# Cross-attention: the layer norm of a group split up and moved into the slots of the group in front, token transposes and Q jobs two slots earlier, residual and context splits moved

## What is computed

```
x = x + attention(layernorm(x))                      # 16 heads of 64, softmax over blocks of 128
x = x + cross_attention(layernorm(x), ctx, ctx, mask)  # 16 heads of 16, keys and values from ctx
x = x + mixture(layernorm(x))                        # 8 experts of 512, summed, gate norm
```

```
Q = x @ Wq.T + bq;  K = ctx @ Wk.T + bk;  V = ctx @ Wv.T + bv
probs = softmax(where(mask, Q K^T / 4, -1e9))
out = (probs V) @ Wo.T + bo
```

## Time and profile before

| | us |
|---|---|
| runs | 952.63, 950.34, 947.82 (median 950.34) |
| the profiled execution | 950.39, of which the trace spans 948.6 |
| cross-attention's first scores | start at 372.56 |
| slot 0 of runs 1, 2, 3 and of the drain (start of S) | 382.76, 429.84, 477.66, 525.71 |
| experts | from about 567 to the end |

### The profile page before, as it was taken

How to read it: one execution, slowest core, us unless ns; L and a number is a source line. 1 busy time by engine, 2 the same in 40 slices (tenths; PEclk the granted TensorE clock), 3 DMA queues, 4 the chain that set the end, 5 groups by cost and what they waited for, 6 DMA issues and landing times.

```text
span 948.6 us, 18374 instructions
## 1 busy us (share of the span) xinstructions
PE 871.0 (92%) x6274; PEld 785.1 (83%) x6274; DVE 567.2 (60%) x1172; ACT 629.4 (66%) x1764; POOL 290.9 (31%) x342
## 2 busy tenths in 40 slices
PE   4899999999999987888988869999999999999997
PEld 3788888889888876787878769999999999999996
DVE  4798888788878865858686856554323332342222
ACT  3797788788778764878787876765454445444543
POOL 2254454445345567546564541000000000000000
PEclk9999999999999999999999999999999999999999
DMA  6310000000000007554444303330000000000000
GB/s 212 105 36 20 1 1 1 0 0 0 0 0 0 1 1 187 114 148 99 144 79 139 75 16 103 92 93 12 22 0 0 0 22 0 0 0 23 1 1 22
DMA packets 21770, 41.98 MB, mean 44 GB/s; under 512 B 3144, under 2 KB 3152, under 8 KB 21712
## 3 DMA queue, kind: packets, MB, share of 16 engines
q1 hardware_dynamic: 21120, 40.91, 16.0%
q10 hardware_dynamic: 592, 0.34, 0.2%
HBM read 30.75 MB, written 10.49 MB: 43 GB/s over the span
## 4 chain that ended last, share of the span: by engine, by line
PE 61%; DVE 17%; ACT 12%; issue 4%; DMA 4%; SPq 1%; POOL 0%; DVEq 0%; ACTq 0%; POOLq 0%
PE Y L482 22%; PE A L482 20%; PE S L482 12%; ACT probs L795 7%; DVE PT L872 3%; PE T L577 3%; DVE nm L962 3%; DVE oraw L981 2%; DVE arena L931 2%; DMA arena<-stage 2%; DMA stage<-arena 1%; DVE st L876 1%; PE O L482 1%; PE O L594 1%; DVE xn L898 1%
## 5 line engine op out<-in xcount | busy, mean ns | idle before, releaser
L872 DVE TENSOR_TENSOR PT<-probs,PT 128x512 fp32r<-128x512 f32 x128 | 89.6, 700 | 231.0 <-ACT PT L852 231.0
L482 PE MATMUL A<-XT,arena 128*128 128x512 f32 x816 | 218.4, 402 | 6.8 <-DVE arena L931 5.5
L795 ACT ACTIVATE probs<-S,nm 128x128 f32<-128x128 f32 x512 | 180.9, 371 | 46.7 <-DVE nm L962 45.1
L482 PEld LDWEIGHTS Y<-arena,PT 128*128 128x128 f32 x1536 | 200.3, 191 | 11.0 <-DVE PT L872 1.1
L482 PE MATMUL Y<-arena,PT 128*128 128x256 f32 x1536 | 204.1, 283 | 0.3
L1185 POOL TENSOR_TENSOR probs<-probs,rinv 128x512 f32<-128x512 f32 x128 | 133.2, 1041 | 215.5 <-DVE rinv L967 213.0
L482 PEld LDWEIGHTS A<-XT,arena 128*128 128x128 f32 x816 | 145.3, 191 | 36.9 <-DVE arena L931 12.4
L852 ACT ACTIVATE PT<-probs 128x512 fp32r<-128x512 f32 x128 | 80.8, 631 | 90.7 <-PE Y L482 90.3
L872 DVE TENSOR_TENSOR PT<-T,PT 128x512 fp32r<-128x512 f32 x128 | 87.6, 684 | 33.9 <-ACT PT L803 31.4
L795 ACT ACTIVATION_READ_ACCUMULATOR probs<-S,nm 128x1 f32 x512 | 107.5, 210 | 0.0
L962 DVE TENSOR_REDUCE nm<-S 128x4 f32<-128x512 f32 x128 | 87.8, 686 | 28.0 <-PE S L569 16.3
(11 more groups left out here) (106 smaller groups left out, 1297.1 us busy)
## 6 DMA issues: line engine op xcount, KB each, us to landing
wst<-in_pieces SPq DMA_DIRECT2D x52, 256.0 KB, 2.7
stage<-arena SPq DMA_DIRECT2D x32, 256.0 KB, 2.3
arena<-stage SPq DMA_DIRECT2D x48, 128.0 KB, 4.0
arena<-stage SPq DMA_DIRECT2D x24, 256.0 KB, 3.8
xs<-in_x SPq DMA_DIRECT2D x4, 512.0 KB, 5.2
craw<-in_ctxT SPq DMA_DIRECT2D x4, 512.0 KB, 3.9
out<-craw SPq DMA_DIRECT2D x4, 512.0 KB, 2.6
rowc<-in_rows ACTq DMA_DIRECT2D x1, 264.0 KB, 5.5
```

The source lines that it names most:

```text
L482: mm = pe.matmul(acc, lhs[a], rhs[b], start=first and i == 0, stop=last and i == 2, skip_group_check=shared)
L795: last = act.activation(probs[:, n % 4, u * P:(u + 1) * P], S[n % 2][:, u * P:(u + 1) * P], ACT.Exp, bias=nm[:, n % 4, u:u + 1], accum_out ...
L872: dve.tensor_tensor(out_, src, hi.bitcast(F32), ALU.subtract).then_inc(sem_, 1)
```

## The change

Tables in the functions `steps` and `run` only, and a `tiles` argument in `stats` and `ln_apply`. For groups 1 to 3 of the cross-attention and for group 0 of the experts:

- statistics: two tiles in slot 10 and two in slot 11 of the run in front (before: four in slot 0); aggregation and the power in its slot 12; `xn` for two tiles in its slot 15 and for two in slot 0 (before: four in slot 1).

For groups 1 to 3 of the cross-attention:

- the token transposes in slots 2 and 3 (before 3 and 5); Q for heads 0 to 7 in slots 4 and 5 (6 and 7), Q for heads 8 to 15 in 6 and 7 (8 and 9), the first half of K for heads 8 to 15 in slot 8 (10), its second half as before in 11.

And: the residual of groups 0 to 2 in slot 7 of the run two further on (before slot 2), its bias in slots 9 and 10 (before 2 and 3); the context split in slots 11 to 14 (before 12 to 15).

```diff
@@ tables @@
-               {0: (0, (0,)), 1: (0, (1,)), 6: (1, (0,)), 7: (1, (1,)),
-                8: (2, (0,)), 9: (2, (1,)), 10: (3, (0,)), 11: (3, (1,))})
+               {0: (0, (0,)), 1: (0, (1,)), 4: (1, (0,)), 5: (1, (1,)),
+                6: (2, (0,)), 7: (2, (1,)), 8: (3, (0,)), 11: (3, (1,))})
-        XT1 = ((3, 4), (3, 5))
+        XT1 = ((3, 4), (2, 3))
+        ALL = tuple(range(TILES))
+        STATS1 = ({0: ALL}, {-6: ALL[:2], -5: ALL[2:]})
+        AGGR1 = (0, -4)
+        NORM1 = ({1: ALL}, {-1: ALL[:2], 0: ALL[2:]})
+        RESIDUAL1 = (QUADS + 6, QUADS + 1)
@@ steps @@
+                at = QUADS - 1 if ph == 0 else RESIDUAL1[g == GROUPS - 1]
+                part = v - SCORES[ph] - at - ((2, 0)[g == GROUPS - 1] if ph == 1 else 1)
+            ahead = ph == 2 or ph == 1 and g > 0
+            if name in ("stats", "norm"):
+                tiles = (STATS1 if name == "stats" else NORM1)[ahead]
+                return [(tiles[v],)] if v in tiles else []
+            if name == "aggr":
+                return [()] if v == AGGR1[ahead] else []
-                return [(g + 1, v - 12)] if ph == 1 and g + 1 < GROUPS and 12 <= v < 16 else []
+                return [(g + 1, v - 11)] if ph == 1 and g + 1 < GROUPS and 11 <= v < 15 else []
@@ run and attentions @@
-                            + [(ph, g, n)]:
+                            + [(ph, g, n)] + [(*e, n - PERIOD) for e in later]:
-            run(order, does, 1, 0, ((0, GROUPS - 1),))
-            run(order, does, 1, 1, ((1, 0),))
-            for g in range(2, GROUPS):
-                run(order, does, 1, g, ((1, g - 1), (1, g - 2)))
+            run(order, does, 1, 0, ((0, GROUPS - 1),), later=((1, 1),))
+            for g in range(1, GROUPS):
+                run(order, does, 1, g, ((1, g - 1), (1, g - 2))[:g],
+                    later=((1, g + 1) if g + 1 < GROUPS else (2, 0),))
```

More of the change, by code:

```diff
@@ L284, in steps @@
                         17: [(1, (2, 3))]}.get(q, [])
[L285 to L293, removed]
+            if name in ("residual", "bias"):
+                at = QUADS - 1 if ph == 0 else RESIDUAL1[g == GROUPS - 1]
+                if name == "residual":
+                    return [()] if v - SCORES[ph] == at else []
+                part = v - SCORES[ph] - at - ((2, 0)[g == GROUPS - 1] if ph == 1 else 1)
+                return [(part,)] if 0 <= part < 2 else []
+            ahead = ph == 2 or ph == 1 and g > 0
[4 more added lines that the diff above has]
+                return [()] if v == AGGR1[ahead] else []
             if name in ("xt0", "xt1"):
@@ L299, in steps, with run @@
             if name == "ctx":
-                return [(g + 1, v - 12)] if ph == 1 and g + 1 < GROUPS and 12 <= v < 16 else []
+                return [(g + 1, v - 11)] if ph == 1 and g + 1 < GROUPS and 11 <= v < 15 else []
             raise ValueError(name)
-        def run(order, does, ph, g, earlier, slots=PERIOD):
+        def run(order, does, ph, g, earlier, slots=PERIOD, later=()):
             for n in range(slots):
@@ L887, in ln_finish, with ln_apply @@
                 dve.tensor_scalar(ve[:, :], mv[:, :, 1], LN_EPS, None, ALU.add).then_inc(ln_var, 1)
-            def ln_apply(ph, g):
+            def ln_apply(ph, g, tiles):
                 dve.wait_ge(ln_rstd, nth(GRP, ph, g, 0))
@@ L893, in ln_apply @@
                     dve.wait_ge(xt_ps, nth(XTE, ph, g, -1))
-                for t in range(TILES):
+                for t in tiles:
                     tile_ = g * TILES + t
@@ L899, in ln_apply @@
                                              ALU.subtract, ALU.mult)
-                last.then_inc(ln_x, 1)
+                if tiles[-1] == TILES - 1:
+                    last.then_inc(ln_x, 1)
             def tokens_lo(ph, g, banks, halves=range(KD)):
@@ L1001, in add_residual, with stats @@
                 last.then_inc(y_read, 1)
-            def stats(ph, g):
+            def stats(ph, g, tiles):
                 if ph == 0:
@@ L1145, in experts @@
                         if m == 28:
-                            ln_apply(2, g + 1)
+                            ln_apply(2, g + 1, range(TILES))
                 if not last:
```

## The result

| | us | |
|---|---|---|
| before | 951.49 (947.82 to 952.95, 4 runs) | |
| after | 938.23 (937.62 to 939.49, 4 runs) | ratio 0.9868, interval 0.9836 to 0.9900 |
| profiled execution after | 937.62, span 935.8 | before 950.39, span 948.6 |

The change makes the kernel about 1.3% faster. The forecast was 934 us, its range 930 to 941: the sign and the range held, and of the 16.5 us that the sum promised the two profiled executions show 12.8.

A forecast was written before the change was run, and what follows sets the result against it. No engine bounds it throughout; some 5 us per run are waits: Q's DRAM trip, layer norm, context. Gains 5.2, 5.0 and 5.25 in runs 1 to 3, drain 2.4, start -1.3: 950.4 - 16.5 = 933.9 us, range 930 to 941.

The forecast's parts named there:

- the DRAM wait: Slot 11's scores wait for Q's 7.8 us trip through DRAM; moved earlier, the wait goes with 2.2 us to spare.
- the lists: Slot prices of TensorE and ScalarE for slots 0 to 15; the larger of each pair sums to 42.3 us a run.
- `xn` in two halves: VectorE, slots 15 and 0: 0.66 us each replaces 1.39 in slot 1, behind the V part in slot 0; costs nothing.
- the context's 0.64: Slot 0: TensorE's K job waits 0.64 us for GpSimd's last context split; moving the split a slot earlier removes it.
- Theory A: Formed after the result: Q's trip is nearly the whole gain; layer norm, V's low part and context split cap slots 0-2 nearly equally.
- The start: Slots 12 to 15 of run 0: power and statistics delay first normalisations (at most 1.6 us) and second maxima; charged 1.3 us.
- The signs: Profile after: no DRAM wait, runs of 42 to 44.3, drain slots 0-2 under 8 us, run 0's first T about 1.3 later.
- rival 1: Transposes and Q halves wait, up to 0.9 us in slot 3, about 0.6 in slots 4, 5; 937 to 938.5; chance 0.23.
- rival 2: Q's DRAM landing grows from 7.8 to 12 us, wait and low clock return, 2.8 a run; 942 us; chance 0.06.
- rival 4: Slower: key and query copies queue on SP, landing doubles to 16 us, a run takes 49.6; 955 us; chance 0.05.
- Rival 3: Slots do not shorten: VectorE's new work in slots 7 and 10-12 delays the maxima; about 945 to 948 us; chance 0.06.
- The rule that I set aside: GpSimd and VectorE's two-port mode exclude each other; `xn` would wait, some 0.25 us each beyond cover, giving 935 us.

The follow-up runs named there:

- Experiment 2: Changed kernel with layer norm, residual and context back in old slots, only Q jobs and token transposes earlier; 938.42 us against 948.98 for the kernel before (0.9886).
- Experiment 9: Changed kernel with transposes, Q and K's first half moved one slot earlier than before instead of two; 941.49 us against 949.9 for the kernel before (0.9912).
- experiment 10: Changed kernel with V ahead of exponentials, aggregation and power in slot 11, group 1's layer norm in its own run; 933.36 us against 949.9 before (0.9830).
- experiment 11: Kernel of experiment 10 with ScalarE's output copy also ahead of the four exponentials; 933.98 us against 949.6 for the kernel before (0.9836).
- experiment 3: Changed kernel with aggregation and power one slot earlier, in slot 11 instead of 12; 938.74 us against 948.98 for the kernel before (0.9891).
- experiment 4: Changed kernel with V's high part ahead of ScalarE's exponentials, its low part ahead of VectorE's output and maxima; 934.69 us against 948.98 before (0.9852).
- experiment 6: Kernel of experiment 4 with the context split back in slots 12 to 15; 935.78 us against 949.9 for the kernel before (0.9852).
- experiment 7: Kernel of experiment 4 with layer norm back in slots 0 and 1; 936.61 us against 949.11 for the kernel before (0.9866).
- experiment 1: Changed kernel with Q jobs and token transposes back in their old slots; 947.17 us against 948.98 for the kernel before (0.998).
- experiment 8: Changed kernel with residual and bias back in their old slots; 937.71 us against 949.6 for the kernel before (0.9874).
- experiment 5: Changed kernel with group 1's layer norm kept in its own run; 936.58 us against 949.9 for the kernel before (0.9861).

## Why the prediction was right, and where it was off

**Right: the DRAM wait and its share.** It was named as the first cap, it is gone from all three runs, and slots 10 to 12 of run 2 went from 11.36 to 7.83. Experiment 2 shows that the queries' half alone gives the result; of some 4.1 us a run 0.7 is slot 9, which lost its second half job, as the lists had it. The lower clock behind the wait went with it, as said. The spare time was near what I gave. In run 2 of the changed kernel Q's low part ends at 447.21, the last copy back lands at 455.22, and the scores of slot 11 start at 457.03: 9.8 us from Q to the scores and 8.0 for the trip (10.0 and 7.8 claimed), so 1.8 to spare against 2.2; in runs 1 and 3 it is 1.8 and 1.3. Experiment 9, which takes a slot away, is 0.63 short in run 1, in accord with it.

**Right in the sum, by luck in its parts: the lists.** Their sum was 42.3 (added up again, 42.4), and experiment 10, with the waits out, has 42.35 and 42.32. Slot 1 was put at 3.1 and slot 2 at 2.83; both are measured to 0.01. Others missed both ways, by 1.25 us up and 1.28 down, and cancelled: the output slots 7, 11 and 15 were put at 2.72 and took 3.0 to 3.06, since O of the next slot waits 0.5 and more for ScalarE's output copy (experiment 11 takes them to 2.55), and slot 5 took 2.64 for 2.4; slots 6, 8 and 12, with a Q or K part, were put at 2.69 and took 2.38, and slot 3 took 3.04 for 3.22. The wait in slots 13 and 14 for aggregation and output, 0.45 by my walk, is 0.48 by experiment 3, all of it in slot 13.

**Wrong: slot 0.** The step that failed is in "`xn` in two halves" and in the list's 2.45 for slot 0: I followed the low part of V on VectorE as something that layer norm stands behind, but not as something that TensorE waits for. O of slot 1 is the first but one to read the new values. The wait was in the trace of before as well, in the open in the drain, where no context split stands in front of it:

```profile
528.27 0.88 PE L482 MATMUL O<-PT,arena 128*32 128x128 f32 x12 [1.25 <-DVE arena L872]
```

In run 2 of before it was hidden by the context's wait, which is of the same height: the low part of V ended at 432.25, O started at 432.40. It is worth 0.83 in runs 2, 3 and the drain, 2.5 of the 4.2 us that are missing in the stage; 1.4 are in slot 0 of run 1 and 0.2 at the start, for other reasons (below). So slots 0 to 3 of a run, which my lists put at 11.6 against 12.77 before, took 12.25, and the drain gave 1.6 in place of 2.4; the context's 0.64 was worth nothing. Experiments 4 and 6 show the two caps on slot 0, experiment 7 that of the layer norm on slots 1 and 2. The layer norm's 0.5 in these slots, less 0.5 in slot 13, came to nothing. Theory A, which put all three on one footing, was wrong in this.

**Off in size: run 1.** I had 41.9, it took 43.26. Its slot 0 lasted 3.88 in place of 2.4, at a granted clock of 0.62 over 384 to 388. The queries' half alone, whose start is as before (10.23) and which does the same work up to there as the kernel before, has 3.77 there at 0.76, where before had 2.36 at 1.00. Nor is it the tables ahead of it: experiments 1, 8 and 9 have those of the changed kernel up to there and took 4.05, 3.28 and 2.73, at 0.57, 0.85 and 0.89, and TensorE has no wait in this slot in any of them. It is when the lower level of the clock (1.2 GHz), which has begun by about 376 in every kernel, ends: at about 385 in experiments 8 and 9, at 387 to 387.5 in the changed kernel and experiment 1. Only experiment 3, whose start is 3 us longer, still has it past 388. What sets the end stays open.

**The start.** 1.3 charged, 1.53 measured, and experiment 5 gives 1.29 of it back. The mechanism was the one named. GpSimd's first normalisation began at 377.89, which is 5.84 behind the first scores against 4.00 before: 1.84 later, more than my bound of 1.6. In experiment 5 it is 0.56 later than before, and the start 0.24 longer.

**The signs.** Two came out a little beside what I had put down: the drain's slots 0 to 2 took 8.05, not under 8, and the first T of run 0 came 1.4 later (6.94 behind the first scores against 5.50), not 1.3.

**The rivals.** The new hand-offs (rival 1) do not show in runs 2 and 3: the first Q half starts at once and slots 2 to 4 exceed the lists by no more than 0.02. In run 1, which has no projections in slots 1 and 2, TensorE is early as I had feared: the second token transposes wait 0.17 for K's low part, and slot 3 lasts 3.37. Rivals 2 and 4 would have needed a longer trip. From the end of Q's low part to the last landing it took 8.0, 8.0 and 8.5 us in runs 1 to 3, against 8.5, 7.8 and 8.0 before. Rival 3 was wrong for this change, though experiment 9 shows a relative of its mechanism one slot away.

**The rule that I set aside.** `xn` was said not to be held up by GpSimd. It is, in its new place. VectorE's timeline after, in slot 15 of run 1 and, for comparison, in slot 15 of run 3, where there is no context split that would push GpSimd's normalisation into it:

```profile
425.44 1.85 DVE L906 TENSOR_SCALAR xn<-xs,mv,rstd 128x256 f32<-128x256 f32 x2
...
512.92 0.73 DVE L906 TENSOR_SCALAR xn<-xs,mv,rstd 128x256 f32<-128x256 f32 x2
```

GpSimd's at the same places:

```profile
424.23 1.30 POOL L1250 TENSOR_TENSOR CT<-craw,CT 128x512 fp32r<-128x512 f32 x1
425.48 1.05 POOL L1194 TENSOR_TENSOR probs<-probs,rinv 128x512 f32<-128x512 f32 x1
...
511.91 1.04 POOL L1194 TENSOR_TENSOR probs<-probs,rinv 128x512 f32<-128x512 f32 x1 [1.71 <-DVE rinv L976]
```

And line 906 from 422 to 431 us (ns min/median/max):

```profile
L906 DVE TENSOR_SCALAR xn<-xs,mv,rstd x4: 402/598/1233, 425.4 to 429.8; 128x256 f32<-128x256 f32 x4
```

1.85 where GpSimd is at work throughout, 0.73 where a normalisation is at its end. The first of the four starts at 425.44, still under the context split, and takes 1.233; its end is 0.15 behind that of the normalisation. The second (from 426.60) takes 0.697 beside an output split that ends at 427.15, the third (from 429.38) 0.498 beside one that ends at 429.73, and each ends 0.15 behind it; the fourth has GpSimd's pause to itself and takes 0.402. The row on which I relied fits as well: of the four `xn` at 436.12 the first took 0.416 and ended 0.15 behind the normalisation at 436.39. So it was held up, but with 0.27 of overlap by no more than 0.01 to 0.02, and it could not speak against the rule. The Trainium skill (SBUF — State Buffer, "SBUF: two separate sides") says that the one of the two that starts first keeps the shared ports for its whole instruction and the other blocks; these ends agree with that. It costs nothing here: VectorE's next low part ends at 427.96, 0.3 before T starts at 428.26, and T has no wait.

## What to carry to other kernels

When several engines' work meets in one slot, ask of each piece not only what is queued behind it on its own engine but who on the other engines waits for it, and how late the second and third of the waits would be. Here V's low part and the context split are two caps of one height on slot 0: with the layer norm moved, taking away either one leaves a run at 43.7 us (the changed kernel and experiment 6), taking away both gives 42.8. A third piece, the layer norm, gave 0.5 us in the slots that it left and cost 0.5 in the slot to which it went. None of the three was taken away quite alone; that stays untested. A sum of slots that comes out right says little on the slots: compare them one by one. Move first what waits once a period for something slow, here a trip through DRAM, and check what already stands in the slot to which it goes. Work that is moved ahead for the steady state also meets the first period, where the queues are filled differently; there it cost 1.5 us, about the gain at the other end (1.6).

## What the runs showed of the hardware

- At the start of the stage TensorE's granted clock falls to the lower level (1.2 GHz, 0.50 to 0.52 over 376 to 380 in every kernel) after a stretch in which it waited for DRAM and then for the exponentials (1.60 and 1.95 in the changed kernel). The stretch 384 to 388 had 1.00 before and 0.50 to 1.00 in the others, and slot 0 of run 1 takes anything from 2.4 to 4.1 us. With the same work up to there it took 2.36 and 3.77 (before and experiment 2), or 2.73 to 4.05 (four kernels). A difference of up to 1.4 us between two profiles may be no more than this.
- A float32 `xn` of 128x256 takes 0.40 us alone. Begun under a GpSimd instruction, it takes 0.40 or ends 0.15 us behind that instruction, whichever is later. In the thirteen traces 93 of 125 such `xn` end 0.15 behind one (to 0.006); the other 32 had less than 0.25 of it left and took 0.40 to 0.41. GpSimd's normalisation hardly changes (1.05 at 425.48, 1.08 at 382.36, 1.04 alone).
- When GpSimd has a second instruction ready right behind the first, the waiting `xn` may have to let that pass too: the one at 425.44 began under the split that ended at 425.53 and finished only behind the normalisation after it, 1.233 in all. At 381.98, at the end of run 0, it got in between (0.569, its end 0.15 behind the split's). What decides is not shown.
- The trip of Q through DRAM, from the end of the low part to the landing of the third copy back, took 7.7 to 8.9 us for heads 0 to 7 in all thirteen traces. For heads 8 to 15, with a low part 5 to 6 us later, it took 8.4 to 10.5.
